# The row maximum's fill ahead of the next tile's scores, in each place of a turn

## The reference

```python
attn = jnp.einsum('bhdm,bhdn->bhmn', q, k) / math.sqrt(head_dim)
attn = jax.nn.softmax(attn, axis=-1)
out = jnp.einsum('bhmn,bhdn->bhdm', attn, v).reshape(b, c, h, w)
out = jnp.einsum('oc,bchw->bohw', proj_w, out) + proj_b[None, :, None, None]
```

## Time and profile before

| | us |
|---|---|
| median of 3 runs | 2105.53 (2100.91 to 2111.38) |
| the profiled execution | 2096.82 |
| its span, first to last instruction | 2095.0 |
| TensorE busy | 1960.1 (94%) |
| VectorE busy | 1440.0 (69%) |
| GpSimd busy | 1118.7 (53%) |
| ScalarE busy | 1045.7 (50%) |
| mean granted TensorE clock | 0.984 of full speed |

### The profile page before, as it was taken

One profiled execution on the slowest core, in us unless ns is written; L12 is line 12 of the kernel. 1 busy time (PEld: TensorE's weight loads), 2 busy tenths in 40 slices (PEclk: granted clock), 3 DMA queues, 4 the chain that ended last, 5 costly groups with the idle time before them and its releaser, 6 DMA issues.

```text
span 2095.0 us, 26308 instructions
## 1 busy us (share of the span) xinstructions
PE 1960.1 (94%) x8072; PEld 1061.8 (51%) x8072; DVE 1440.0 (69%) x1638; ACT 1045.7 (50%) x1346; POOL 1118.7 (53%) x533
## 2 busy tenths in 40 slices
PE   4999999999999999999999989999899999999994
PEld 3555555545555455555555545455554555545431
DVE  5658768486784957758586785857858587685743
ACT  3555545454555444555454555454554455554441
POOL 3665555464555545555464564645555555554660
PEclk9999999999999999999999999999999999999997
DMA  3112131121313012130121312113130121301201
GB/s 137 42 26 82 36 101 26 44 74 31 101 31 96 20 36 91 32 105 20 41 81 31 101 30 65 47 36 96 31 101 18 38 87 34 101 24 43 56 27 61
DMA packets 65694, 119.35 MB, mean 57 GB/s; under 512 B 20480, under 2 KB 21248, under 8 KB 65536
## 3 DMA queue, kind: packets, MB, share of 16 engines
q1 hardware_dynamic: 65664, 118.97, 19.4%
HBM read 54.68 MB, written 17.04 MB: 34 GB/s over the span
## 4 chain that ended last, share of the span: by engine, by line
PE 79%; DVE 12%; issue 5%; DMA 2%; ACT 2%; DVEq 0%; SPq 0%; POOL 0%; ACTq 0%
PE PV L590 19%; PE SB L461 12%; PE S L574 11%; PE MS L555 10%; PE S L577 9%; PE SB L498 5%; PE SB L532 4%; DVE mx L763 4%; DVE mix L854 3%; PE SB L492 3%; PE SB L540 3%; DVE rden L841 2%; PE SB L519 1%; DVE o L836 1%; DVE x_lo L755 1%
## 5 line engine op out<-in xcount | busy, mean ns | idle before, releaser
L447 POOL TENSOR_TENSOR psum_p<-psum_p,prob 128x1024 f32<-128x1024 f32 x384 | 931.1, 2425 | 596.4 <-ACT prob L654 589.0
L763 DVE TENSOR_REDUCE mx<-MS 128x1 f32<-128x1024 f32 x500 | 609.9, 1220 | 416.1 <-PE MS L555 413.9
L654 ACT ACTIVATE prob<-S 128x1024 f32<-128x1024 f32 x512 | 523.7, 1024 | 405.1 <-PE S L577 398.6
L590 PE MATMUL PV<-prob,V 128*64 128x512 f32 x2048 | 506.9, 617 | 0.0
L574 PE MATMUL S<-Q,K 128*128 128x512 f32 x1024 | 455.1, 444 | 2.5 <-DVE mx L910 2.5
L577 PE MATMUL S<-Q,K 128*128 128x512 f32 x1024 | 406.1, 397 | 0.3 <-DMA Q<-mrow 0.3
L555 PE MATMUL MS<-K,Q 128*128 128x512 f32 x1000 | 327.8, 409 | 73.3 <-DVE mx L763 73.2
L574 PEld LDWEIGHTS S<-Q,K 128*128 128x128 f32 x1024 | 194.3, 190 | 264.9 <-issue 231.4
L447 POOL TENSOR_TENSOR psum_p<-prob 128x1024 f32<-128x1024 f32 x64 | 151.7, 2370 | 311.3 <-ACT prob L654 311.3
L590 PEld LDWEIGHTS PV<-prob,V 128*64 128x64 f32 x2048 | 125.5, 137 | 266.4 <-issue 240.5
L555 PEld LDWEIGHTS MS<-K,Q 128*128 128x128 f32 x1000 | 176.5, 188 | 162.5 <-DVE mx L763 131.2
(11 more groups left out here) (126 smaller groups left out, 1879.8 us busy)
## 6 DMA issues: line engine op xcount, KB each, us to landing
xin<-in_x_dram SPq DMA_DIRECT2D x16, 1024.0 KB, 8.7
K<-K SPq DMA_DIRECT2D x128, 128.0 KB, 2.2
Q<-Q SPq DMA_DIRECT2D x128, 128.0 KB, 2.3
rz<-z_dram SPq DMA_DIRECT2D x128, 128.0 KB, 2.9
x<-in_x_dram SPq DMA_DIRECT2D x16, 1024.0 KB, 6.2
out_dram<-y SPq DMA_DIRECT2D x64, 256.0 KB, 2.1
V<-v_next SPq DMA_DIRECT2D x16, 512.0 KB, 6.5
hpad<-hpad SPq DMA_DIRECT2D x16, 289.0 KB, 3.1
```

The source lines that it names most:

```text
L447: nc.gpsimd.tensor_tensor(acc, first_in, prob[:, s % PBUF, :, :], ALU.add).then_inc(add_done, 1)
L590: last = nc.tensor.matmul(PV[own(a), :], V[:, b // NH, kt, a * D:a * D + D], prob[:, s % PBUF, a, :], start=(kt == 0), stop=(kt == KT - 1))
L654: nc.scalar.activation(prob[:, s % PBUF, :, :], S[:, s % 2, :, :], ACT.Exp, scale=D ** -0.5).then_inc(exp_done, 1)
L763: nc.vector.reduce_max(mx[:, b % 2, m:m + 1], MS[:, :, :], AX.XY).then_inc(max_read, 1)
```

## The change

In each place of a turn TensorE's program now calls `max_fill` first and `scores` behind it, then the jobs. The order on the other engines, every wait and every instruction are as they were.

```diff
--- before.py
+++ after.py
@@ -617,13 +617,13 @@
                 held = [("row", 0, 0)] if first else [(kind, i - 1 + di, f)]
                 for t in range(TURNS):
                     for half, place in ((0, MID), (1, LATE)):
+                        at = fill_at(i, 2 * t + half, last)
+                        if at:
+                            max_fill(*at)
                         if t < TURNS - 1:
                             scores(i, 2 * t + 2 + half)
                         elif not last:
                             scores(i + 1, half)
-                        at = fill_at(i, 2 * t + half, last)
-                        if at:
-                            max_fill(*at)
                         for kind, di, f in jobs_of(place, t, first, last):
                             job(kind, i + di, f, held)
                             held = [(kind, i + di, f)]
```

## The result

The kernel with the change takes 2186.57 us (median of 4 runs, 2185.76 to 2187.33), the kernel before 2108.24 in the same comparison: ratio 1.0377 (95% interval 1.0346 to 1.0407), 78.3 us more. Slower was forecast, at 2138 us, which is 32.5 more than the 2105.53 known then. More than twice as much was lost, and 2186.57 lies above the range.

What follows compares the result with a forecast made beforehand. TensorE was taken to bound, except in turns 6 to 10 (VectorE). A, B, C and D sum to 2.45 us per image, 35.5 us over 14.5 images: 2132 or 2141, taken as 2138 us; range 2118 to 2155, 2098 to 2164 with rivals.

Steps and rivals of the forecast that it cites:

- A: Turn 0: fill 1 loses its cover, waits 0.39 us and takes 0.11 longer; 0.5 us per image.
- B: Turns 1 and 2: 0.70 us of fill 4's gain is lost and fill 5 waits; 0.9 us per image.
- C: Turns 3 to 5: loss at fills 8 and 10, given back by gdev finishing before its addition; 0.1 us per image.
- The 0.11 of a waiting fill: Any fill that waits: its two matmuls take 0.73 or 0.74 us instead of 0.62, 0.11 more.
- D: Turns 6 to 10, where VectorE binds: hand sum of late scores and shut-ins through fill 21; 0.95 us per image.
- No change: Rival: waits from fill to fill stay the same and all cancels, 2105 us within 0.5%; 17 in 100.
- Faster, by the shut-ins: Rival: later additions free x_lo and the mix in turns 7 and 8, saving 3.9 us per image: 2083 us; 11 in 100.
- The clock: Rival: TensorE's granted clock falls more behind the longer wait of fill 15, 21 us more: 2160 us; 15 in 100.
- P: Theory of the experiments: scores behind a waiting fill pay its wait on TensorE's path; before, they were done in its shade.
- L: Theory of the experiments: later additions meet other VectorE operations, and which are shut in sets VectorE's time where it binds.

Runs made afterwards that it cites:

- e9: Fill ahead of scores only in the second place of turn 2, old order elsewhere, against the kernel before: 2120.52 us against 2102.38, 1.0079.
- e5: GpSimd's additions cut to 8 of 512 columns, in either order, against the kernel before (2108.59 us): old order 2009.05, new order 2025.98.
- e3: Fill ahead of scores only in turns 0 to 4, old order elsewhere, against the kernel before: 2127.88 us against 2110.09, 1.0085.
- e1: Fill ahead of scores only in the first place of each turn, against the kernel before: 2074.3 us against 2110.09, 0.9835.
- e6: Seven later mixes cut to 8 of 768 columns, in either order, against the kernel before (2108.59 us): old order 2094.01, new order 2118.32.

## Why the prediction was right in kind and wrong in size

**A, turn 0: right.** 0.5 predicted, 0.51 measured; fill 1 waits 0.39 in the mean, start to start.

**B, turns 1 and 2: right.** 0.9 predicted, 1.01 measured, and e9, the second place of turn 2 alone, has 0.93 in that turn. The rule behind both (what the fill gains and the jobs don't give back is waited for) holds. Both rest on the long additions more than the prediction said: without them (e5) turn 0 loses nothing and turn 2 loses 0.37.

**C, turns 3 to 5: right.** 0.1 predicted, 0.08 measured. gdev (L778) fell from a mean of 891 ns to 226, which fits an addition that now comes behind it.

**The 0.11 of a waiting fill: the row was right.** Every waiting fill shown at 2.4 GHz takes 0.73 or 0.74, an unhindered one 0.62. In the changed kernel a fill stands right behind a pv matmul too, and takes 0.73 there without a wait, where the first scores matmul took 0.50 before; so the duration by itself doesn't prove a wait.

**D, turns 6 to 10: this is the step that failed.** 0.95 was predicted for it, 4.03 measured (turns 6 to 11 and 13). The rest, 0.51 + 1.01 + 0.08, makes 1.6 of the 5.6. The prediction expected VectorE's busy time to fall by the shut-ins of x_lo and gdev; it rose by 14.1 us. x_lo did fall (a mean of 2037 ns to 1305), but others are shut in instead: the mixes of L854 went from 1295 to 1651 ns, and o from 1382 to 1741. In the changed kernel:

```profile
L854 DVE SCALAR_TENSOR_TENSOR mix<-ex,rw,mix 128x768 f32<-128x768 f32 x105 | 173.4, 1651 | 1.0
L836 DVE TENSOR_TENSOR o<-o,rz 128x512 f32<-128x512 f32 x64 | 111.4, 1741 | 27.3 <-DMA rz<-z_dram 27.3
```

The hand sum's own stations can be laid beside the traces: the start of each fill counted from fill 12, after less before, and less the 0.93 by which fill 12 itself moved ahead (us, means over images 1 to 14 of after). Of the kernel before, the first line takes the 6 images in which the mix of turn 8 is shut in, as in the image that the prediction worked on, the second line the 8 others.

```
fill                        13     15     17     19     21     23
against 6 images, shut in  0.00   1.23  -0.42  -0.07   0.62   2.43
against 8 images, free     0.00   1.20   0.95   1.41   2.12   3.89
predicted                  0      1.1   -0.6     .      0      .
```

Up to fill 17 the working held within 0.2 for the images of its own kind. Three things make up the missing 3.1:

- *The end of the sum, 1.8 us.* The prediction stopped at fill 21 ("is released at about the old time, with 0.93 of scores behind it"). Those scores' addition was not followed into turn 11, though the prediction had said that exp and addition are late "by the whole wait" behind a waiting fill. From fill 21 to 23 an image loses 1.8 (7.97 to 9.77).
- *The image it was worked on, 0.9 us.* The mix at 1105.62 is shut in, and in 11 of 14 images stays so with the change; but in 8 of 14 images it was free before, as the earlier trace rows showed. Those lose 1.5 more: 8/14 x 1.5 = 0.9. This piece may belong to the profiled pair and not to the medians. The profiled executions of e3 and e9, in which turns 5 to 15 have the old order, have only 4 such free images each. With 4 instead of 8 the kernel before would take 6 us more than its profiled execution, by an estimate, of the 11.4 by which its median is above it. It has one trace, so this stays open.
- *Turns 9 and 10, 0.6 us.* Fill 19, which never waited, waits 0.39 in the mean, and fill 21 2.3 for 1.6 (start to start). It looks like the lost cover of fill 5, which the prediction counted for turns 1 to 5 alone; no run has it by itself.

1.8 + 0.9 + 0.6 less what turn 13 gave back, 0.1 to 0.2, is 3.1 to 3.2. Over the whole kernel 89.7 - 35.5 = 54.2 us are missing in the profiled pair: 3.1 in each of the 14 middle images (43), the rest mostly at the ends. In the medians it is 78.3 - 35.5 = 42.8.

**The rivals.** *No change* assumed that turns 6 to 10 begin and end alike; fill to fill they don't, by the points above. *Faster, by the shut-ins* saw a real effect in the wrong kernel: x_lo did come free, the mix didn't, but e1, which leaves the waiting fills in place, gets a free mix (turn 8 at 8.20 for 9.90) and is 1.65% faster. *The clock* isn't the cause as far as these numbers go. The changed kernel's falls are more (18 in its middle images, 8 before), and elsewhere. Its stretches around turns 7, 10 and 11, of the image of the rows and (last two) of the next, in the columns of the earlier trace rows:

```profile
1143.00:1147.00 4.00, 3.71 (x10) 1.81 (x12) 4.00 (x5) 2.90 (x4) 2.08 (x2) 0.64 0.00 1
...
1178.00:1182.00 4.00, 4.00 (x18) 3.51 (x19) 2.78 (x3) 1.05 (x2) 1.73 (x2) 0.57 0.18 67
1306.00:1310.00 4.00, 2.02 (x10) 1.17 (x9) 3.73 (x6) 1.02 (x1) 1.52 (x2) 1.00 0.30 67
1310.00:1314.00 4.00, 4.00 (x26) 2.77 (x24) 2.45 (x2) 1.69 (x3) 2.41 (x2) 1.00 0.24 67
```

In the first image the clock is at its lower level, 1.2 GHz, for part of the stretch behind fill 13 and behind fill 21, both of which had waited (1.84 and 2.45 us); in the next it stays at 2.4 GHz behind fill 21, which had waited 1.98. From fill 21 to fill 23 the 9 images with a fall there take 9.79 us and the 5 without take 9.71: a price of 0.08. That fits VectorE binding there; the two groups also differ in whether a mix or o is shut in. If all of the lower mean clock (0.974 for 0.984) were lost time it would be 2184.7 x 0.026 - 2095.0 x 0.016 = 23 us of the 89.7 between the two profiled executions; e6 (the new order slower at the higher clock) and e9 (1.0079 at a granted clock of 0.988) show that the order costs time without a lower clock. That the clock costs exactly nothing here wasn't shown, and elsewhere a fall does cost: in turn 10 of e6's old order, where fill 23 doesn't wait, it was 1.0 us.

How much of D is P and how much L stays open. They don't add: a shut-in lengthens a wait, and the wait delays the next addition. e5 only bounds it, for the whole kernel: 17 us without long additions.

## What to carry to other kernels

On an engine that works in order, put work that is ready ahead of an instruction that waits, never behind it; look up for each place whether it waits, since here the same swap gains 1.7% in one half of the places and costs 5.8% in the other. When a place moves, follow its product to the last engine that it disturbs and past the place where the hand sum seems to close, and do it in an image of each kind that the trace holds. Where VectorE and GpSimd exclude each other, measure the margin between their starts: here one of about 0.1 us decided over 2 us.

## What the runs showed of the hardware that was not expected

**A lower clock made an image shorter.** Of the 14 middle images of the kernel before, the 8 in which TensorE's clock fell in turn 7 have the mix of turn 8 free and take 47.4 to 47.7 us for turns 6 to 11; the 6 in which it kept 2.4 GHz have it shut in (3.14) and take 48.9 to 49.0. The earlier trace rows are one of each. That the slow matmuls make the scores and so the addition late enough for the mix to pass is the reading that fits; it wasn't tried by itself. In the profiled executions of e3 and e9 the 6 middle images with a fall in turn 7 have this mix free too; of the 22 without one, 20 have it shut in and 2 have it free. And it isn't so everywhere: in e6's old order a fall made turn 10 longer.

**Who starts first wins, and the loser pays a tail.** At 1146.68 o ran first and the addition of 1146.73 took 2.87 for 2.38; the mix behind it, begun at 1147.28, ended at 1150.41, 0.81 behind the addition's end. The Trainium skill, "SBUF — State Buffer", section "SBUF: two separate sides", says that a VectorE operation with two SBUF inputs and a GpSimd operation that reads SBUF exclude each other for the whole instruction, whichever starts first. The trace agrees. The 0.81 goes beyond that rule, and the recorded starts don't decide below 0.1 us: a mix that began 0.08 us behind an addition's start took 0.92 (1124.87, the kernel before), and one of 8 columns that began 0.07 behind took 2.30, and at most 0.23 where it was free (1123.72, e6's old order).
